# A row of logits made as a column and spread over the partitions through DRAM, in place of a matmul against a widened weight

## The reference

```python
# layer 1: eight heads of 16, masked softmax attention, then Wo and bo
scores = einsum('bhqd,bhkd->bhqk', q, k) / sqrt(16)
ctx    = einsum('bhqk,bhkd->bhqd', softmax(where(adj > 0, scores, -1e9)), v)
x = layernorm(x + ctx @ Wo + bo)
# layer 2: graph attention with additive logits
h   = einsum('bsf,of->bso', x, W)
f_i = h @ a[0, :128]
f_j = h @ a[0, 128:]
e   = f_i[:, :, None] + f_j[:, None, :]
e   = where(e >= 0, e, 0.2 * e)
att = softmax(where(adj > 0, e, -9e15), axis=2)
x = layernorm(x + einsum('bij,bjo->bio', att, h))
```

## Time and profile before

| | |
|---|---|
| median of three runs | 891.87 us |
| the profiled execution | 889.27 us, span 887.3 us |
| mean granted clock of PE | 0.977 |
| PE, DVE, ACT busy | 818.8, 698.0, 702.3 us |
| job fi: PE line 579 | 32 matmuls, 15.0 us |
| job fi: ACT line 719 | 8 copies, 8.2 us |
| jobs atts: DVE line 859 | 64, 83.2 us |

### The profile page before, as it was taken

One profiled execution on the slowest core, in us unless ns is written; L12 is line 12 of the kernel. 1 busy time (PEld: TensorE's weight loads), 2 busy tenths in 40 slices (PEclk: granted clock), 3 DMA queues, 4 the chain that ended last, 5 costly groups with the idle time before them and its releaser, 6 DMA issues.

```text
span 887.3 us, 19518 instructions
## 1 busy us (share of the span) xinstructions
PE 818.8 (92%) x7647; PEld 400.1 (45%) x7680; DVE 698.0 (79%) x1141; ACT 702.3 (79%) x766; POOL 118.1 (13%) x92
## 2 busy tenths in 40 slices
PE   6399999989999999999999999999999999998982
PEld 4023334425643365334643357333653356433861
DVE  5288679797788978988788977988878987788473
ACT  2399899999779977899779986899769996898050
POOL 4000100030012010031001120132000220122030
PEclk9599999999999999999999999999999999999997
DMA  4656617441266135452365224661363422401001
GB/s 148 147 158 174 132 62 191 152 87 49 96 175 146 39 100 128 129 124 63 106 169 149 37 78 143 156 133 37 107 166 117 90 85 85 96 2 49 1 13 39
DMA packets 51779, 92.16 MB, mean 104 GB/s; under 512 B 3729, under 2 KB 20882, under 8 KB 51666
## 3 DMA queue, kind: packets, MB, share of 16 engines
q1 hardware_dynamic: 51682, 90.85, 38.8%
HBM read 67.63 MB, written 23.20 MB: 102 GB/s over the span
## 4 chain that ended last, share of the span: by engine, by line
PE 69%; ACT 15%; issue 9%; DVE 5%; POOL 0%; POOLq 0%; ACTq 0%; DVEq 0%
PE acc L474 18%; PE slot L509 12%; ACT weights L632 11%; PE slot L441 9%; PE slot L450 9%; PE slot L520 3%; PE slot L446 3%; PE slot L453 2%; ACT atts L658 2%; PE slot L557 2%; DVE x L920 2%; PE slot L571 2%; PE slot L547 2%; PE slot L579 2%; PE slot L491 1%
## 5 line engine op out<-in xcount | busy, mean ns | idle before, releaser
L632 ACT ACTIVATE weights<-slot 128x1024 f32<-128x1024 f32 x504 | 491.8, 1040 | 75.8 <-PE slot L450 38.0
L844 DVE SCALAR_TENSOR_TENSOR weights<-mask,weights 128x1024 f32<-128x1024 bf16 x336 | 403.4, 1236 | 52.8 <-ACT weights L632 42.7
L474 PE MATMUL acc<-weights,vst 128*17 128x512 f32 x2048 | 243.6, 594 | 0.0
L441 PE MATMUL slot<-qst,kst 97*32 97x512 bf16 x2240 | 160.5, 383 | 5.8 <-ACT weights L632 5.2
L450 PE MATMUL slot<-qst,kst 97*128 97x512 bf16 x464 | 133.6, 389 | 25.7 <-issue 13.8
L509 PEld LDWEIGHTS slot<-hst,atts 128*128 128x128 f32 x896 | 106.8, 191 | 17.4 <-ACT weights L632 9.6
L509 PE MATMUL slot<-hst,atts 128*128 128x129 f32 x896 | 110.5, 276 | 3.2 <-issue 1.7
L474 PEld LDWEIGHTS acc<-weights,vst 128*17 128x17 f32 x2048 | 52.3, 97 | 119.8 <-issue 96.8
L441 PEld LDWEIGHTS slot<-qst,kst 97*32 97x32 bf16 x2240 | 49.5, 95 | 116.0 <-ACT weights L632 49.3
L859 DVE SCALAR_TENSOR_TENSOR atts<-turn,hst,mask 128x1024 f32<-128x1024 f32 x64 | 83.2, 1323 | 21.5 <-DMA k_scratch<-atts 15.2
L781 POOL TENSOR_TENSOR rstd<-vareps,exponent 128x4 f32<-128x4 f32 (+1 forms) x24 | 29.3, 1222 | 468.3 <-DVE vareps L915 468.3
(11 more groups left out here) (135 smaller groups left out, 683.5 us busy)
## 6 DMA issues: line engine op xcount, KB each, us to landing
raw<-in_adjT SPq DMA_DIRECT2D x64, 512.0 KB, 3.6
q_scratch<-atts SPq DMA_DIRECT2D x48, 256.0 KB
qst<-q_scratch SPq DMA_DIRECT2D x16, 768.0 KB
k_scratch<-atts SPq DMA_DIRECT2D x24, 256.0 KB
kst<-k_scratch SPq DMA_DIRECT2D x16, 384.0 KB
xT_sb<-in_xT SPq DMA_DIRECT2D x8, 512.0 KB, 4.4
kst<-k_scratch SPq DMA_DIRECT2D x16, 256.0 KB
x_sb<-in_x SPq DMA_DIRECT2D x8, 512.0 KB, 4.7
```

The source lines that it names most:

```text
L441: mm = pe.matmul(ps[rows, cols], kst[:, h, keys], qst[:, h, cols], start=True, stop=not by_pe)
L474: mm = pe.matmul(acc[VW * i:VW * i + HD + 1, cols], vst[b % 2][:, t, g * HG + i], weights[:, HG * buffer(b, n) + i, cols], start=(t == 0), ...
L632: act.activation(to, ps[:], ACT.Exp, scale=SCALE).then_inc(exp_done, 1)
L844: dve.scalar_tensor_tensor(out=to, in0=masks[b % 2][:, n % T], scalar=0.0, in1=at, op0=ALU.is_equal, op1=ALU.mult).then_inc(masked, 1)
```

## The change

For all batches but the last, job `fi` is gone from PE and ACT. `wh` gets one more column, 0.8 f_i; it arrives in `hst` with h, one value for each node, eight to a partition. SP sends that column to a row of 1024 floats in DRAM (`send_fi`, 1024 pieces of 4 bytes) once both halves of h are there, waits until it has landed, and reads the row back to all 128 partitions (`spread_fi`, 512 KB written). DVE waits for that before `atts0`. The last batch keeps the matmul. `h0` moves from position 32 to 30, `h1` from 39 to 33, `atts0` and `atts1` from 35 and 38 to 42 and 44, `exp0` from 40 to 45, and others by a few.

```diff
 SP_AT = {
-    20: [("stackk1", 0)], ... 30: [("partsk", 1), ("shift", 1)], 31: [("raw1", 1)], 35: [("stackq0", 1)], ...
+    19: [("raw7", 0), ("stackk1", 0)], ... 30: [("partsk", 1), ("shift", 1)],
+    31: [("raw1", 1)], 33: [("fiout", -1)], 34: [("fiin", -1)], 35: [("stackq0", 1)], 37: [("stackr0", 1)],
 PE_AT = {
-    ... 3: [("out7", -2)], ...
-    30: [("cc", 1)], 32: [("h0", -1)], 35: [("fi", -1)], 39: [("h1", -1)],
+    ... 2: [("out7", -2)], ...
+    30: [("cc", 1), ("h0", -1)], 33: [("h1", -1)], 38: [("fi", -1)],
 ACT_AT = {
-    30: [("cc", 1)], 32: [("h0", -1)], 35: [("fi", -1)], 36: [("acc0", 0)], 39: [("h1", -1)],
-    40: [("exp0", -1)], 45: [("exp1", -1)], 48: [("exp2", -1)], 52: [("exp3", -1)], 54: [("exp4", -1)],
+    30: [("cc", 1), ("h0", -1)], 33: [("h1", -1)], 36: [("acc0", 0)], 38: [("fi", -1)],
+    45: [("exp0", -1)], 48: [("exp1", -1)], 49: [("exp2", -1)], 52: [("exp3", -1)], 54: [("exp4", -1)],
 DVE_AT = {
-    35: [("atts0", -1)], 38: [("atts1", -1)], 42: [("atts2", -1)], 45: [("atts3", -1)],
-    46: [("atts4", -1), ("h1", -1)], 54: [("atts5", -1)], 56: [("atts6", -1), ("norm2", -2)], 58: [("atts7", -1)],
+    38: [("h1", -1)], 42: [("atts0", -1)], 44: [("atts1", -1)], 46: [("atts2", -1)], 49: [("atts3", -1)],
+    52: [("atts4", -1)], 54: [("atts5", -1)], 56: [("norm2", -2), ("atts6", -1)], 58: [("atts7", -1)],
...
+            def send_fi(b):
+                sp.wait_ge(taken["h0"], b + 1)
+                sp.wait_ge(taken["h1"], b + 1)
+                sp.wait_ge(fi_in, b * 16)
+                with nc.allow_non_contiguous_dma(reason="a column of hst"):
+                    sp.dma_start(fi_scratch[0].rearrange("(t p) -> p t", p=128), hst[:, :, HW - 1]).then_inc(fi_out, 16)
+
+            def spread_fi(b):
+                sp.wait_ge(fi_out, (b + 1) * 16)
+                sp.wait_ge(full["wo"], b + 1)
+                sp.dma_start(fi_all[:], fi_scratch.to_broadcast([128, N])).then_inc(fi_in, 16)
...
-                    dve.wait_ge(taken["fi"], b + 1)
+                    if b == B - 1:
+                        dve.wait_ge(taken["fi"], 1)
+                    if b < B - 1:
+                        dve.wait_ge(fi_in, (b + 1) * 16)
...
+                act.activation(wh[:, D + 2:D + 3], acc[:, 256:257], ACT.Copy, scale=1.0 - ALPHA)
```

More of the change, by code:

```diff
@@ L31 @@
 SP_AT = {
[3 rows of a table removed]
+    2: [("xT", 1)], 8: [("stackr1", 0)], 16: [("raw5", 0)], 17: [("raw6", 0)], 19: [("raw7", 0), ("stackk1", 0)],
+    22: [("stackq1", 0)], 23: [("raw0", 1)], 26: [("partsq", 1)], 30: [("partsk", 1), ("shift", 1)],
+    31: [("raw1", 1)], 33: [("fiout", -1)], 34: [("fiin", -1)], 35: [("stackq0", 1)], 37: [("stackr0", 1)],
     40: [("stackk0", 1), ("store0", -2)], 42: [("x", 0), ("raw2", 1)], 51: [("raw3", 1)], 52: [("raw4", 1)],
@@ L95, in ring_plan @@
             uses += [(name, me, 0) for name, me in jobs_at(PE_AT, b, pos, batches)
-                     if not (me == batches - 1 and name[:3] == "out")]
+                     if not (me == batches - 1 and name[:3] == "out") and not (me < batches - 1 and name == "fi")]
     slot = {use: i % 3 for i, use in enumerate(uses)}
@@ L121, in build_fast @@
     SROWS = KROWS + 1
-    HW = D + 3
+    HW = D + 4
     VW = 32
@@ L156, in build_fast @@
         acol = sb("acol", [D, 2], F32)
-        wh = sb("wh", [D, D + 2], F32)
+        wh = sb("wh", [D, D + 3], F32)
         uwide = sb("uwide", [D, D], F32)
@@ L227, in build_fast @@
         k_scratch = nc.dram_tensor("k_scratch", [H, 3, HD, N], BF16, kind="Internal").ap()
+        fi_scratch = nc.dram_tensor("fi_scratch", [1, N], F32, kind="Internal").ap()
         flag_scratch = nc.dram_tensor("flag_scratch", [1, 128], I32, kind="Internal").ap()
@@ L274, in build_fast @@
         out_done = [sem(f"out{i}_done") for i in range(2)]
+        fi_out = sem("fi_out")
+        fi_in = sem("fi_in")
         too_far_made = sem("too_far_made")
@@ L293, in released @@
             if job != "unit":
-                return taken[job], b + 1
+                return taken[job], 1 if job == "fi" else b + 1
             if MASKED_BY[n] == "d":
@@ L382, in job @@
                     load_x(me)
+                elif name in ("fiout", "fiin"):
+                    if me < B - 1:
+                        (send_fi if name == "fiout" else spread_fi)(me)
                 elif name[:5] == "parts":
@@ L511, in job @@
                     return
+                if name == "fi" and me < B - 1:
+                    return
                 ps = slot_of(name, me)
@@ L569, in job @@
                         u = 4 * int(name[1]) + t
-                        at = t // 2 * HALF + t % 2 * (D + 2)
-                        mm = pe.matmul(ps[:, at:at + D + 2], x1T[:, u * 128:(u + 1) * 128], wh[:], **kw)
+                        at = t // 2 * HALF + t % 2 * (D + 3)
+                        mm = pe.matmul(ps[:, at:at + D + 3], x1T[:, u * 128:(u + 1) * 128], wh[:], **kw)
                     if name == "h1":
-                        at = HALF + 2 * (D + 2)
+                        at = HALF + 2 * (D + 3)
                         mm = pe.matmul(ps[0:SUMS, at:at + D], x1sum[:].to_broadcast([D, SUMS]), wh[:, 0:D], **kw)
@@ L669, in job @@
                     return
+                if name == "fi" and me < B - 1:
+                    return
                 ps = slot_of(name, me)
-                act.wait_ge(full[name], me + 1)
+                act.wait_ge(full[name], 1 if name == "fi" else me + 1)
                 if name in ("q", "k"):
@@ L709, in job @@
                         act.wait_ge(full[f"out{t}"], me)
-                    view = ps[:].rearrange("p (k w) -> p k w", k=2)[:, :, 0:2 * (D + 2)]
+                    view = ps[:].rearrange("p (k w) -> p k w", k=2)[:, :, 0:2 * (D + 3)]
                     ins = act.activation(hst[:, 4 * k:4 * k + 4, 1:HW].rearrange("p (k t) w -> p k t w", k=2),
@@ L898, in divide_contexts @@
                 dve.wait_ge(full["h1"], b)
-                dve.wait_ge(full["fi"], b)
                 link(dve.reciprocal(rden[:, tt], view[:, :, :, HD]))
```

## The result

The changed kernel takes **948.06 us** in the median of four runs (944.63 to 949.18), beside 891.38 (888.39 to 896.82) for the kernel before, in four. The ratio is 1.0625, with a 95% interval of 1.0595 to 1.0656: 6.3% slower. The forecast was 932 with a range to 948; so the sign and the mechanism came out as forecast, the loss is 57 us where 42 and 1.3 were summed, and the time stands at the very end of the range.

What follows compares the result with a forecast made beforehand. ACT was taken to bound each batch's second stretch, where atts0 waits for the row. 889.3 + 42 (6.0 us late in seven batches) + 1.3 (last batch) = 932.6, given as 932 us, range 879 to 948.

Steps and rivals of the forecast that it cites:

- What bounds it, and what ACT wins: From position 37 to batch end ACT is busy without a gap; at best 0.9 us a batch is won.
- rival (c): PE limits all through; fi's 1.72 us come off each of seven batches, transfers hidden: 878.6 us; chance 0.16.
- The column: SP's write to DRAM, issued at 277.4 behind raw1, is out at 282.6 + 5.7 = 288.3 us.
- the flags: Traced write of 128 4-byte pieces to one DRAM row, landed 7.6 us after issue; taken as the column's price, 5.7.
- rival (a): Small writes land like a plain store; atts0 0.7 to 2.1 us late a batch, 896 to 905 us; chance 0.21.
- The count: 1024 pieces against the flags' 128: eight times the number need not cost eight times as much.
- Rival (d): Worse: writes follow one another, 972 us at 12 us, over 1200 at eight times; or PE's clock, 953; chance 0.10.
- The read back: Broadcast of the row, 512 KB: 3.6 us as a raw block; the only broadcast read, bo_all, took 5.0.
- The sum of a batch: atts0 done at 293.2, 6.4 us late by ACT's date, 5.6 by DVE's; middle 6.0, times seven is 42.
- What would show it: Broadcast issued 10 to 11 us after the column, DVE idle some 7, ACT as long, PE beside it, batch 108.
- Rival (d)'s clock: PE idles some 4 us a batch, falls to half speed for 8 us, costing some 3 us a batch: 953 us.
- The last batch: fi runs behind h1, so DVE's eight atts start behind PE's 1.3 us of h1: +1.3 us in full.

Runs made afterwards that it cites:

- free row: Changed kernel without the two transfers or any wait for them; DVE reads a stale row in batches 0 to 6: 890.3 us, 0.9998 of the kernel before.
- six experiments between the free row and the turned version: Changed kernel with write alone 907.7, read alone 901.16, 32-byte pieces 935.09, transfers earlier in queue 925.82, pieces 64 bytes apart 911.8, an eighth of pieces 939.44 us.
- turned version: Changed kernel, column transposed on PE, written as 8 pieces of 512 bytes, both issues ahead of raw1, old order in last batch: 892.18 us, 1.0012.
- order alone: Changed kernel's order of jobs without transfers; all eight batches make the row by the matmul of fi, at position 38: 900.56 us, 1.0123.
- both turned versions: Changed kernel with the column transposed on PE and written as 512-byte pieces, without and with 12 extra matmuls before the last out matmuls: 892.18 and 891.22 us.
- free row with the filled gap: Changed kernel without transfers or wait, row stale, plus 15 extra matmuls on PE before the last out matmuls: 886.12 us, 0.9941.

## Why the prediction was right, and where its sizes were off

- **What bounds it, and what ACT wins.** Confirmed. The best case was 0.9 us a batch if the row cost nothing; the free row wins 0.7. With the row free and 1.7 us of PE gone the time is 890.3 and not 878.6 (the median span 886.4): rival (c), PE as the limit all through, is excluded, although PE's share of 92% speaks for it.
- **The column.** Forecast: landed 10.9 us after its issue (277.4 to 288.3), as 5.2 behind raw1 and 5.7 of its own by the flags. Measured: 12.5 to 14.8 in the six loaded batches, 10.0 alone. The flags were the right row. What was wrong is the split: the 10 us are the write's own, and a queue in front of it adds 1 to 5 rather than setting the date. This is the largest mis-sized term: 13.7 against 10.9 in the batch shown, 2.8 us. The Trainium skill, "DMA: Bandwidth & Descriptors", section "Anatomy of one DMA", puts a DMA's fixed cost down to the completion, since its last step waits for the data to be written, and says that this can take surprisingly long when the target is HBM. The seventh row agrees, with 8.4 us between the last packet and the next issue. That section describes DMAs issued by GpSimd, and SP issues these, so its figure of about 2 us, named beside rival (a), was not made for them. It is near the measured times of the pieces of 32 and 512 bytes (1.4 and 1.2) and of those set apart (2.9), and far from the packed pieces of 4 bytes (7.9 and 10.0).
- **The count.** "Eight times the number need not cost eight times as much" was right: 7.9 us for 128, 10.0 for 1024. Rival (d)'s writes one after another is excluded by that.
- **The read back.** Forecast 3.6; measured 4.0 to 4.9, median 4.7, between the two rows. It adds 0.4 to 1.3 us a batch.
- **The sum of a batch.** From the column's issue to the end of the first sum 15.8 us were forecast and 19.2 came (283.59 to 302.83), so 3.4 more. Not all of it was paid: a batch is 8.4 us longer than before where 6.0 was forecast, and the seventh only 3.0. That is 52.0 over the seven, where the sum had 42.
- **What would show it.** All four marks are there, each somewhat long: the broadcast 13.7 us behind the column, not 10 to 11; DVE idle 8.2, not 7; ACT idle 6.4 and PE 5.7 beside it; a batch of 110.6, not 108.
- **Rival (d)'s clock.** It was half right: PE does fall to 0.50, for 7 us in two of the batches and for 10 in the other five, but without the price of 3 us. In six of the seven ACT, which bounds that stretch, has no wait in it behind the first exponential of the attention; in the last it has one, 0.8 us for PE.
- **The last batch.** Forecast +1.3; measured +5.2 (4.7 on the free row). The step counted PE's and ACT's instructions ahead of the first sum, and not what a longer gap does to PE's clock behind it. Of the 4.7 us on the free row, 2.0 pass before the last out matmuls start (1.1 of them the longer gap, 3.96 against 2.85), and the half-speed groups are 1.3 + 0.5 + 0.7 = 2.5. Filling the gap took 2.4 us off the tail (79.1 against 81.5).

So the step that decided was right, and the error of 15 us is two terms: the write's landing with the read (10 us over seven batches) and the tail (4). The rest, 1.7 us, is time around the span, which the sum took over from before as 2.0: it is 3.7 in this execution (948.25 less 944.5).

**What stays open.** Why the write of the column holds up PE's own instruction stream (the 1.06 us gap above) is not shown; that the transfers compete with the fetching of instructions is only a guess. Nor is it shown what sets the time around the span. It is 3.2 to 4.4 us in every run of the changed kernel, of the free row and of the six experiments between the free row and the turned version, with the old order of the tail on the free row too; and it is 1.8 to 2.0 in every run of the kernel before, of the order alone, of both turned versions and of the free row with the filled gap. It does not follow the clock in the tail, which falls in the turned version as well.

## What to carry to other kernels

A small result that has to change its layout through DRAM is priced by the landing of the write and not by its bytes: look for pieces of 4 bytes that are neighbours in DRAM (pieces of 32 bytes were fast already), and turn the data on chip first. Here 0.3 us of PE and 0.25 of ACT a batch, with both issues moved up in the queue, took back the 57 us. Before building such a change, make the thing free (a stale row, no wait) and time it: here that one run gave 890.3 against 890.0, so no transfer, however fast, had anything to win in this order of jobs. Compare the spans as well as the times: 1.6 us of gain were hidden behind 2.1 us outside the span. And look at the last batch by itself: a gap that was 1.1 us longer in front of the final matmuls was followed by 2.5 us of slower matmuls.

## What the runs showed of the hardware that was not expected

- Writes of 4 bytes that share 64 bytes of DRAM are signalled complete 8 to 10 us after issue on an empty queue (128 pieces 7.9, 1024 pieces 10.0), though the packets of the 1024 are over in 1.6 us. The 1024 pieces 64 bytes apart: 2.9. As 32-byte pieces: 1.4. As 512-byte pieces: 1.2.
- The read of the row that follows them is later too. In the unloaded seventh batch it landed 4.4 to 5.1 us after its issue behind a packed column (three executions), and 3.3 to 3.8 where the write before it was set apart, in pieces of 32 or 512 bytes, or absent (five).
- 4 KB written so, with nobody waiting for the row, cost 2.5 us a batch; the trace shows it as a later landing of other DMAs and as breaks in PE's instruction stream.
- DVE's sum takes 2.1 us where it reads the row of fp32 with a step of 32 bytes, and 1.28 with unit stride.
- An idle of 3.20 or 3.96 us in front of PE's last matmuls was followed by a granted clock of 0.50 for 3 to 7 us, an idle of 2.85 us by none; 3.2 us of work without use in the gap kept it at 1.00.
